# Second attention of a two-layer kernel: mask fused with the row maximum, transposes in three groups, GpSimd divides by the sums

## What is computed

```python
y = jnp.einsum('bnd,hde->bhne', x, Wkqv) + bkqv[None, :, None, :]      # 16 heads
k, q, v = y[..., :Dm], y[..., Dm:2 * Dm], y[..., 2 * Dm:]              # k, q: 128 wide; v: 8 wide
A = jnp.einsum('bhnd,bhmd->bhnm', q, k) / jnp.sqrt(jnp.float32(Dm))
A = jnp.where(mask[None, None], A, -jnp.inf)                           # causal
A = jax.nn.softmax(A, axis=-1)
sa = jnp.einsum('bhnm,bhmd->bnhd', A, v).reshape(Bm, Nm, Dm)
```

## Time and profile before

| | us |
|---|---|
| median of three runs | 2656.59 |
| the profiled execution | 2639.07 |
| its span | 2637.3 |
| PE busy | 2377.5 (90%) |
| DVE busy | 1886.6 (72%) |
| ACT busy | 1562.1 (59%) |
| POOL busy | 1022.7 (39%) |
| the loop of the second attention, 256 steps | about 1315, or 5.15 a step |

### The profile page before, as it was taken

One profiled execution on the slowest core, in us unless ns is written; L12 is line 12 of the kernel. 1 busy time (PEld: TensorE's weight loads), 2 busy tenths in 40 slices (PEclk: granted clock), 3 DMA queues, 4 the chain that ended last, 5 costly groups with the idle time before them and its releaser, 6 DMA issues. The chain is left out here.

```text
span 2637.3 us, 67465 instructions
## 1 busy us (share of the span) xinstructions
PE 2377.5 (90%) x17172; PEld 1690.3 (64%) x17173; DVE 1886.6 (72%) x5258; ACT 1562.1 (59%) x4145; POOL 1022.7 (39%) x1980
## 2 busy tenths in 40 slices
PE   5999999987999999999999999999989964999970
PEld 3676777765666666666666666666657753777750
DVE  6888888844777777777777777777744553666658
ACT  2555555554777777777777777777743322444445
POOL 5666666651222222222222222222215664444432
PEclk9999999998999999999999999999975556999985
DMA  1101111101000000000000000000041111111125
GB/s 31 32 25 32 32 32 32 32 19 37 0 0 0 0 0 0 0 0 0 0 0 0 0 0 0 0 0 0 0 119 64 61 58 46 52 53 51 52 66 160
DMA packets 78015, 71.60 MB, mean 27 GB/s; under 512 B 10621, under 2 KB 70538, under 8 KB 77084
## 3 DMA queue, kind: packets, MB, share of 16 engines
q1 hardware_dynamic: 69262, 53.65, 7.0%
q0 software_dynamic: 8704, 17.39, 2.0%
HBM read 36.32 MB, written 22.62 MB: 22 GB/s over the span
## 5 line engine op out<-in xcount | busy, mean ns | idle before, releaser
L887 PE MATMUL ps_s<-xT_all,qm 128*128 (+2 forms) x2048 | 695.9, 448 | 0.8 <-ACT qm L955 0.8
L1005 DVE SCALAR_TENSOR_TENSOR restT<-ps_t,leadT 128x512 f16<-128x512 f32 (+3 forms) x1024 | 498.3, 487 | 259.9 <-ACT leadT L970 259.9
L970 ACT ACTIVATE leadT<-ps_t 128x512 f16<-128x512 f32 (+3 forms) x1024 | 422.4, 441 | 311.2 <-PE ps_t L901 311.1
L962 ACT ACTIVATE p<-ps_s,neg_max 128x512 f32<-128x512 f32 (+3 forms) x1024 | 483.3, 525 | 32.8 <-DVE neg_max L997 4.6
L997 DVE TENSOR_REDUCE neg_max<-ps_s 128x1 f32<-128x512 f32 (+3 forms) x1024 | 471.4, 481 | 30.6 <-PE ps_s L889 30.6
L901 PE MATMUL ps_t<-ident,p 128*128 128x128 f32 x2560 | 416.8, 277 | 19.3 <-issue 17.4
L887 PEld LDWEIGHTS ps_s<-xT_all,qm 128*128 128x128 f32 x2048 | 309.9, 191 | 156.5 <-issue 118.7
L840 POOL CAST v_parts<-v_all 128x36 bf16 (+1 forms) x256 | 56.5, 221 | 875.6 <-PE ps_o L913 875.6
L901 PEld LDWEIGHTS ps_t<-ident,p 128*128 128x128 f32 x2560 | 278.9, 141 | 179.6 <-issue 179.4
L879 PE MATMUL ps_qm<-xT_all,m_head 128*128 (+1 forms) x512 | 271.7, 612 | 0.5 <-ACT mb_all L947 0.5
L266 POOL TENSOR_TENSOR pv_prod<-probs,kv 128x2048 f32<-128x2048 f32 x64 | 259.6, 4079 | 0.1
(11 more groups left out here) (216 smaller groups left out, 4196.6 us busy)
## 6 DMA issues: line engine op xcount, KB each, us to landing
row_in<-rows_dram SPq DMA_DIRECT2D x136, 64.5 KB, 1.8
y<-results SPq DMA_DIRECT2D x32, 256.0 KB, 3.3
xT<-in_xT SPq DMA_DIRECT2D x32, 128.0 KB, 2.1
xres<-in_xT SPq DMA_DIRECT2D x32, 128.0 KB, 2.1
x_all<-x SPq DMA_DIRECT2D x32, 128.0 KB, 2.0
xT_all<-x2T SPq DMA_DIRECT2D x32, 128.0 KB, 2.0
x_all<-x SPq DMA_DIRECT2D x16, 256.0 KB, 2.5
out_x<-x SPq DMA_DIRECT2D x16, 256.0 KB, 2.2
```

Source lines behind the costliest of these rows:

```text
L887: pe.matmul(ps_s[i][:, 0:n], qm[j][:, i * P:n], xT_all[:, bass.ds(sequence(u) * S, n)], start=True, stop=False)
L962: act.activation(probs[i][:, :], ps_s[i][:, 0:(i + 1) * P], ACT.Exp, bias=neg_max[:, i:i + 1]).then_inc(probs_ready[i], 1)
L970: act.activation(leadT[i][:, :], ps_t[i % 2][:, 0:(i + 1) * P], ACT.Copy, scale=RAISE)\
L1005: dve.scalar_tensor_tensor(out=restT[i][:, :], in0=ps_t[i % 2][:, 0:(i + 1) * P], scalar=RAISE, in1=leadT[i][:, :], op0=ALU.mult, op1=ALU. ...
```

## The change

- `scores` drops the mask product (L889). Block 1 and block 0 go into one bank and signal once, after block 0.
- `row_max` becomes `mask_and_max`: one `tensor_tensor_reduce` on VectorE adds a float32 mask from SBUF to the scores in PSUM, multiplies by -1, writes the result back into PSUM and gives the minimum of it. The exponentials read it with scale -1.
- The ten transposed blocks form three groups: block 3 (512 columns), blocks 2 and 0 (512), block 1 (256). Groups 0 and 2 share a bank. There are three lead copies and three rests in place of four. Their order on PE, ACT and DVE changes.
- The output has one semaphore, after its last block, in place of four.
- VectorE keeps the sum of the parts. GpSimd takes the division: a power of -1 of the four row sums, then the product into `sa_all`. It does so in step k for pair k-1, after `split_values` of k+1. `out_sum` has two buffers.

```diff
                 def step(u, j, nxt, last, this):
                     if nxt:
                         load_head(*before(u, j, -1))
                         split_values(*before(u, j, -1))
+                    if last:
+                        divide(*before(u, j, 1))
...
+                def divide(u, j):
+                    k = 2 * u + j
+                    sums = out_sum[j][:, :].rearrange("p (i c) -> p i c", c=PV)
+                    wait_alone(pool, out_summed, k + 1, passed)
+                    when(pool, out_ready, k)
+                    pool.tensor_tensor(recip[:, :], sums[:, :, DH], minus_one[:, :], ALU.pow).then_inc(recips_ready, 1)
+                    pool.wait_ge(recips_ready, k + 1)
+                    pool.tensor_tensor(sa_steps[:, bass.ds(k, 1), :, :].rearrange("p k i c -> p (k i) c"),
+                                       sums[:, :, 0:DH], recip[:, :].unsqueeze(2).to_broadcast([P, B, DH]),
+                                       ALU.mult).then_inc(out_ready, 1)
...
-                    pe.matmul(ps_s[i][:, 0:n], qm[j][:, i * P:n], xT_all[:, bass.ds(sequence(u) * S, n)],
-                              start=True, stop=False)
-                    pe.matmul(ps_s[i][:, i * P:n], ident16[:, :], mask16[:, :], start=False, stop=True)\
-                        .then_inc(scores_ps[i], 1)
+                    for n in ((1, 0) if i == 1 else (i,)):
+                        when(pe, probs_ready[n], k)
+                        mm = pe.matmul(ps_s[n], qm[j][:, n * P:(n + 1) * P],
+                                       xT_all[:, bass.ds(sequence(u) * S, (n + 1) * P)], start=True, stop=True)
+                    mm.then_inc(scores_ps[i], 1)
...
                     if last:
-                        turn(*b, 3)
-                        turn(*b, 2)
+                        turn(*b, 0)
                     if this:
                         scores(u, j, 3)
+                    if last:
+                        turn(*b, 1)
+                    if this:
                         scores(u, j, 2)
                     if last:
-                        turn(*b, 1)
+                        turn(*b, 2)
                     if nxt:
                         queries(*before(u, j, -1))
-                    if last:
-                        turn(*b, 0)
                     if this:
                         scores(u, j, 1)
-                        scores(u, j, 0)
                     if last:
-                        for i in reversed(range(B)):
-                            weighted_values(*b, i)
+                        weighted_values(*b)
...
-                    dve.tensor_reduce(neg_max[:, i:i + 1], ps_s[i][:, 0:(i + 1) * P], AX_X, ALU.max,
-                                      negate=True).then_inc(max_ready[i], 1)
+                    dve.tensor_tensor_reduce(out=ps_s[i], in0=ps_s[i], in1=mask[:, S - n:S],
+                                             scale=-1.0, scalar=3e38, op0=ALU.add, op1=ALU.min,
+                                             accum_out=neg_max[:, i:i + 1]).then_inc(max_ready[i], 1)
...
-                    dve.wait_ge(out_summed, k + 1)
-                    dve.reciprocal(recip[:, :], sums[:, :, DH]).then_inc(recips_ready, 1)
-                    dve.wait_ge(recips_ready, k + 1)
-                    dve.tensor_tensor(sa_steps[:, bass.ds(k, 1), :, :].rearrange("p k i c -> p (k i) c"),
-                                      sums[:, :, 0:DH], recip[:, :].unsqueeze(2).to_broadcast([P, B, DH]),
-                                      ALU.mult).then_inc(out_ready, 1)
```

More of the change, by code:

```diff
@@ L755, in attention1 @@
         probs = [sb(f"p{i}", [P, (i + 1) * P]) for i in range(B)]
-        leadT = [sb(f"leadT{i}", [P, (i + 1) * P], F16) for i in range(B)]
-        restT = [sb(f"restT{i}", [P, (i + 1) * P], F16) for i in range(B)]
+        groups = ((3,), (2, 0), (1,))
+        width = [sum(i + 1 for i in group) * P for group in groups]
+        group_of = {3: (0, 0), 2: (1, 0), 0: (1, 3 * P), 1: (2, 0)}
+        leadT = [sb(f"leadT{g}", [P, n], F16) for g, n in enumerate(width)]
+        restT = [sb(f"restT{g}", [P, n], F16) for g, n in enumerate(width)]
         v_parts = [sb(f"v_parts{j}", [P, B * PARTS * PV], BF16) for j in range(2)]
         v_rest = sb("v_rest", [P, B * PV])
-        out_sum, recip = sb("out_sum", [P, B * PV]), sb("recip", [P, B])
-        ps_s = [ctx.enter_context(nc.psum_tensor(f"ps_s{i}", [P, S], F32)) for i in range(B)]
-        ps_t = [ctx.enter_context(nc.psum_tensor(f"ps_t{i}", [P, S], F32)) for i in range(2)]
+        out_sum = [sb(f"out_sum{j}", [P, B * PV]) for j in range(2)]
+        recip, minus_one = sb("recip", [P, B]), sb("minus_one", [P, B])
+        ps_low, ps_s2, ps_s3, ps_t0, ps_t1 = (
+            ctx.enter_context(nc.psum_tensor(name, [P, S], F32)) for name in ("ps_low", "ps_s2", "ps_s3", "ps_t0", "ps_t1"))
+        ps_s = (ps_low[:, 2 * P:3 * P], ps_low[:, 0:2 * P], ps_s2[:, 0:3 * P], ps_s3[:, :])
+        ps_t = (ps_t0, ps_t1, ps_t0)
+        ps_m = (ps_low, ps_s2, ps_s3, ps_t0)
         ps_qm = ctx.enter_context(nc.psum_tensor("ps_qm", [P, S], F32))
@@ L817, in _ @@
             def _(pool):
[L818 to L823, removed]
+                pool.memset(mask[:, :], 0.0).then_inc(consts_zeroed, 1)
+                pool.memset(minus_one[:, :], -1.0).then_inc(consts_zeroed, 1)
+                pool.wait_ge(consts_zeroed, 2)
+                pool.affine_select(out=mask[:, 3 * P:4 * P], in_=mask[:, 3 * P:4 * P], compare_op=ALU.is_ge,
+                                   fill=MASKED, base=0, pattern=[[-1, P]], channel_multiplier=1)\
+                    .then_inc(consts_made, 1)
                 pool.wait_ge(m_sb, H // 4)
@@ new lines, in scores, with turn @@
+                    mm.then_inc(scores_ps[i], 1)
+                def turn(u, j, g):
+                    k = 2 * u + j
+                    if g == 0:
+                        when(pe, rest_ready[2], k)
+                    if g == 1:
+                        when(pe, rest_ready[1], k)
+                    if g == 2:
+                        pe.wait_ge(rest_ready[0], k + 1)
+                    for i in groups[g]:
+                        pe.wait_ge(probs_ready[i], k + 1)
+                        at = group_of[i][1]
+                        for n in range(i + 1):
+                            mm = pe.transpose(ps_t[g][:, at + n * P:at + (n + 1) * P], probs[i][:, n * P:(n + 1) * P],
+                                              ident[:, :])
+                    mm.then_inc(pT_ps[g], 1)
@@ new lines, in weighted_values @@
+                def weighted_values(u, j):
+                    k = 2 * u + j
+                    pe.wait_ge(v_parts_ready, 3 * (k + 1))
+                    when(pe, out_summed, k)
+                    for i in (3, 2, 0, 1):
+                        g, at = group_of[i]
+                        pe.wait_ge(rest_ready[g], k + 1)
+                        for n in range(i + 1):
+                            for part in (leadT[g], restT[g]):
+                                mm = pe.matmul(out_ps[:, i, :], part[:, at + n * P:at + (n + 1) * P],
+                                               v_parts[j][:, n * PARTS * PV:(n + 1) * PARTS * PV],
+                                               start=(n == 0 and part is leadT[g]), stop=(n == i and part is restT[g]))
+                    mm.then_inc(out_ready_ps, 1)
@@ L953, in copy_queries @@
                     act.wait_ge(qm_ps, k + 1)
-                    when(act, scores_ps[0], k - 1)
+                    when(act, scores_ps[1], k - 1)
                     act.activation(qm[j][:, :], ps_qm[:, :], ACT.Identity,
@@ L975, in step @@
                     if last:
[L976 to L977 removed]
+                        copy_lead(*b, 0)
                         copy_lead(*b, 1)
@@ L980, in step @@
                         exponentials(u, j, 3)
+                    if last:
+                        copy_lead(*b, 2)
+                    if this:
                         exponentials(u, j, 2)
-                    if last:
-                        copy_lead(*b, 0)
                     if nxt:
@@ L993, in _, with mask_and_max @@
             def _(dve):
[L994 removed]
+                dve.wait_ge(consts_made, 1)
+                def mask_and_max(u, j, i):
                     k = 2 * u + j
[L996 to L1007 removed]
@@ L1025, in step @@
                     if last:
-                        take_rest(*b, 3)
+                        take_rest(*b, 0)
                     if this:
-                        row_max(u, j, 3)
+                        mask_and_max(u, j, 3)
+                    if last:
+                        take_rest(*b, 1)
+                    if this:
+                        mask_and_max(u, j, 2)
                     if last:
@@ L1031, in step @@
                     if this:
-                        row_max(u, j, 2)
+                        mask_and_max(u, j, 1)
+                        mask_and_max(u, j, 0)
                     if last:
[L1034 to L1037, removed]
```

(4 more changed lines are left out.)

79 lines of the change are left out of this document (32 added, 47 removed).

## The result

The changed kernel took 2817.05 us (median of four runs, 2813.45 to 2818.33) against 2654.52 us for the kernel before (four runs, 2650.73 to 2658.57). The ratio is 1.0609, with a 95% interval of 1.0588 to 1.0631: slower by 6.1%, 163 us. The forecast was 2792.

A forecast was written before the change was run, and what follows sets the result against it. TensorE's own stream was taken to set the step. The division would delay GpSimd's `m_head` copy: 5.62 + 0.06 = 5.68 us against 5.15, +0.53 x 255 = +135, so 2656.6 + 135 = 2792 us; range 2685 to 2860.

The forecast's parts named there:

- The circle: Loop from TensorE's transposes through GpSimd's cast, split, division and `m_head` copy to the query product; 5.62 us a step, 5.68 with loop end.
- The main step: GpSimd's queue: the division, 1.44 us, stands ahead of the `m_head` copy, which has only 0.6 us to spare.
- the 2.30: TensorE, before the change: us from the query product to the end of its step; 2.00 after taking off one transpose and masks.
- rival 1: GpSimd's division: power of -1 as cheap as a plain operation (0.26 us), step 4.90 us, gain 64 us, 2593; chance 0.11.
- rival 3: GpSimd's division: power nearer 0.69 us and gap 0.08, step 5.24 us, +23 us, 2680; chance 0.07.
- No gap in them is left to fill: TensorE's 5.07 us between step starts: its own stream sets the step, so masks off it would save 0.36 us.
- rival 2: VectorE: the fused maximum runs at half rate, 4.9 us busy a step, +179 us, 2835; chance 0.06.
- the bound of 0.19: VectorE's fused maxima: each up to 0.19 us dearer if reading the accumulator costs what it costs on ScalarE.
- Waits of TensorE for a rest: Sign against the forecast, on TensorE: it would wait for a rest or an exponential; no size given.
- the stall of 1.0 us: TensorE before the query product: stands still about 1.0 us in each step, waiting for the `m_head` copy.
- The 4.7 us for a step without the wait: Sign for the forecast: TensorE's step, leaving out its wait for the `m_head` copy, is 4.7 us.
- rival 4: TensorE's clock: idle 18% of a step, it could fall to 1.2 GHz, kernel over 3600 us; chance 0.03.

## Why the prediction was right, and where it was not

**The circle.** The main step held: the division stands ahead of the copy, the copy has 0.6 us of slack, and the division is longer. The copy comes 2.84 us after its cast, 1.48 later than before, as the division's 1.44 said. Four steps in a row, read from the timelines (the step starts with its query product):

| us | query product to cast | cast to power | power to copy | copy to next query product | step |
|---|---|---|---|---|---|
| from 1202.69 | 2.53 | 1.40 | 1.44 | 0.47 | 5.84 |
| from 1208.53 | 2.54 | 1.34 | 1.38 | 0.34 | 5.60 |
| from 1214.13 | 2.53 | 1.34 | 1.44 | 0.47 | 5.78 |
| from 1219.91 | 2.54 | 1.34 | 1.68 | 0.35 | 5.91 |
| mean | 2.54 | 1.36 | 1.49 | 0.41 | 5.78 |
| predicted | 2.42 | 1.36 | 1.44 + 0.06 | 0.40 | 5.68 |

The last of the four has GpSimd's loop end, on the path as predicted:

```profile
1225.47 0.29 POOL L836 COPY m_head<-m_all 128x128 f32 x1 [0.25 <-issue]
```

One term is mis-sized, the way from the query product to the next cast, by 0.12 us. Most of it is the query product itself. After the wait, from 1202.69 to the next scores, it takes 0.96 us. In the step of the earlier trace rows from which I took the 2.30, it took 0.87, from 1200.41 to this row of the kernel before:

```profile
1201.28 0.27 PE L901 MATMUL ps_t<-ident,p 128*128 128x128 f32 x1
```

The other query product in the earlier trace rows takes 0.93, so the 0.87 was also the shorter of two steps. The other three terms are right to 0.01 us on average, so the forecast does not come near through errors that cancel. Two slips in the working change nothing: VectorE at half rate comes to 4.83 us and not 4.9, and the chances of the slower outcomes add up to 0.87 and not 0.86.

**The power.** All 256 powers of the changed kernel:

```profile
L862 POOL TENSOR_TENSOR recip<-out_sum,minus_one x256: 1002/1006/1032, 635.1 to 2103.9; 128x4 f32<-128x4 f32 x128
```

The exponent -1 is hardly cheaper than -0.5: 1.006 us against the 1.042 of the earlier trace rows. With this, rivals 1 and 3 fall. The Trainium skill ("GPSIMD Engine Reference", section 3.1) gives `tensor_tensor` about 2.6 cycles an element on GpSimd, which at the 1.2 GHz of the same section is an estimate of 0.002 us. That does not hold for a power: from two elements (0.69 us) to four (1.04) it grows by 0.17 us for each.

**TensorE's gain.** "No gap in them is left to fill" was the step that failed. It is true of the starts and yet does not mean that TensorE alone sets the step. I priced the masks at 0.36 us and said that the step would be 4.71. The run without masks gained 0.07: the slots were worth 0.34, and waits took 0.27 of it. The last rest alone had 0.06 us of slack in one step and 0.13 in the next, and I had not followed it. The error did not touch the forecast, because the longer circle covered it. It would have spoilt rival 1, which I put at 4.90 us: the three runs that bring the copy forward came to 5.05.

**VectorE.** That the fused form runs at the maximum's rate was right for 512 columns (0.69 and 0.68 us), and nearly so for 128 (0.33 and 0.28), so rival 2 falls. Its accumulator read costs 0.14 us:

```profile
L1023 DVE DVE_READ_ACCUMULATOR2_ANT neg_max<- x1024: 140/141/145, 625.4 to 2099.6; 128x1 f32 x171
```

This lies within the bound of 0.19 from the earlier trace rows. The Trainium skill ("VectorE: DVE Perf Modes", "Two Vector instructions with no wait between them") says that an operation that also writes out its accumulator is two instructions. The trace agrees: each of the 1024 fused instructions has its read. In the changed kernel nothing shows that they cost time; in the run with the fused form alone ScalarE waits for one of them in each step.

**What I said would prove me wrong.** "Waits of TensorE for a rest" was on that list, and there are 143 us of them. They stand ahead of the third group's transposes, in the stall of 1.0 us that I had forecast. In the run with the division on VectorE the same wait is still there (107.6 us in 228 steps) and the step is 5.05 us all the same, so it was covered in the changed kernel. As a sign it was badly chosen: a wait inside a longer wait says nothing. Of the signs for being right, one holds in part: TensorE's idle time before the query product's weight load is 0.8 us and not 1, because the wait for the rest takes its share of the stall. The 4.7 us for a step without the wait never came; it was 5.05.

**The clock.** It stayed at 1.00 of the full level with TensorE idle in a tenth of the stretch (1072 of 1200 us busy); rival 4 did not come. In the run with two powers, where TensorE was busy 881 of 1150 us, single short falls to the lower level did come, at a cost of 0.07 us a step.

## What to carry to other kernels

Before work is moved to an idle engine, look at what follows it in that engine's queue and who waits for that: here an engine idle three quarters of the time had 0.6 us to spare, and one line of order decided between 6% slower and 0.6% faster. A moved operation goes behind everything that others wait for. And an engine that is busy 99% of the time does not say what its relief is worth: read how late its inputs come in, since the next wait can lie 0.1 us below.

## What the runs showed of the hardware

A power of four elements on GpSimd takes 1.0 us with exponent -1 as with -0.5, and 0.7 us for two elements; VectorE's reciprocal of four elements takes 0.18. The query product, two float32 passes over 512 columns, takes 0.96 us after an idle TensorE and 0.86 in the run where nothing is awaited ahead of it, both at the full clock. The read of a VectorE accumulator (0.14 us) starts together with the next instruction and so costs VectorE hardly anything, but whoever needs its value waits for it.
